# Ten tiles in two groups: the fourth output row of a tile is written directly behind the first, ahead of the second half of the next planes, and the last product of each of the two phases goes to another pair of PSUM banks

## What is computed

```
out = conv3x3_decomposed(x, lsq_quantize(w1, alpha1))
out = relu(batchnorm(out, gamma1, beta1))
out = conv3x3_decomposed(out, lsq_quantize(w2, alpha2))
out = batchnorm(out, gamma2, beta2)
out = relu(out + residual)          # residual = x
```

## Time and profile before

| | |
|---|---|
| median of three runs | 1582.2 us |
| the profiled execution | 1582.83 us, span 1580.7 us |
| phase 1 | to about 645 us |
| phase 2 | from about 645 to 1270 us |
| last stage | from about 1270 us on, DMA 99% busy |
| busy over the span | DVE 1196.5, PE 1112.5, ACT 842.3, POOL 497.5 us |
| granted TensorE clock | 0.887 of full speed over the span, 1.00 from 160 to 610 us and from 760 to 1260 us, 0.50 from 60 to 64 us and from 124 to 128 us |

### The profile page before, as it was taken

One profiled execution on the slowest core, in us unless ns is written; L12 is line 12 of the kernel. 1 busy time (PEld: TensorE's weight loads), 2 busy tenths in 40 slices (PEclk: granted clock), 3 DMA queues, 4 the chain that ended last, 5 costly groups with the idle time before them and its releaser, 6 DMA issues.

```text
span 1580.7 us, 22063 instructions
## 1 busy us (share of the span) xinstructions
PE 1112.5 (70%) x6954; PEld 1058.9 (67%) x6954; DVE 1196.5 (76%) x2074; ACT 842.3 (53%) x1135; POOL 497.5 (31%) x219
## 2 busy tenths in 40 slices
PE   5788998999999999579889999999989900000000
PEld 5787888888888888578888888888888900000000
DVE  7898998888888887688888888888888662323234
ACT  3454555555555555466766777776676552222224
POOL 2343334444433334133344444333344300000000
PEclk9998999999999999799999999999999955555555
DMA  4244444444442220001134444444222199999999
GB/s 191 84 164 161 164 163 163 163 163 180 181 182 107 81 81 1 1 41 82 81 122 163 163 183 180 177 184 189 103 81 81 51 419 430 429 430 430 430 430 407
DMA packets 28103, 296.89 MB, mean 188 GB/s; under 512 B 3888, under 2 KB 3888, under 8 KB 4784
## 3 DMA queue, kind: packets, MB, share of 16 engines
q1 hardware_dynamic: 22608, 245.25, 39.3%
q10 hardware_dynamic: 5472, 51.38, 7.6%
HBM read 174.59 MB, written 122.03 MB: 188 GB/s over the span
## 4 chain that ended last, share of the span: by engine, by line
DVE 42%; DMA 16%; PE 14%; issue 10%; DVEq 3%; ACT 2%; POOL 0%; POOLq 0%; ACTq 0%
PE conv_psum L942 13%; DMA slots<-conv_spill 10%; DVE slots L764 10%; DVE q_rows L696 8%; DVE v_rows L733 4%; DVE p_rows L721 4%; DVE d_lo L737 3%; DMA out<-slots 3%; DMA xbuf<-in_x 3%; DVE conv_psum L756 3%; DVE d L696 2%; DVE v_rows L696 2%; DVE slots L923 1%; DVE v_rows L717 1%; DVEq L764 1%
## 5 line engine op out<-in xcount | busy, mean ns | idle before, releaser
L454 POOL TENSOR_TENSOR v_lo<-v_rows,v_hi 128x1120 fp32r<-128x1120 f32 x192 | 494.9, 2592 | 751.8 <-ACT v_hi L513 751.8
L942 PE MATMUL conv_psum<-v_hi,w1T 128*128 128x284 f32 x1152 | 314.4, 301 | 69.2 <-DVE slots L764 62.5
L942 PE MATMUL conv_psum<-v_hi,w2T 128*128 128x284 f32 x1152 | 312.2, 299 | 66.5 <-DVE slots L764 58.9
L942 PE MATMUL conv_psum<-v_lo,w1T 128*128 128x284 f32 x1152 | 311.7, 299 | 0.0
L942 PE MATMUL conv_psum<-v_lo,w2T 128*128 128x284 f32 x1152 | 309.5, 297 | 0.0
L942 PEld LDWEIGHTS conv_psum<-v_hi,w1T 128*128 128x128 f32 x1152 | 222.0, 193 | 76.4 <-issue 70.5
L942 PEld LDWEIGHTS conv_psum<-v_hi,w2T 128*128 128x128 f32 x1152 | 220.7, 192 | 73.4 <-issue 63.2
L526 ACT COPY m<-conv_psum 128x568 f32<-128x568 f32 x128 | 81.3, 635 | 297.6 <-PE conv_psum L942 297.6
L556 ACT ACTIVATE squares<-slots,minus_shift 128x1120 bf16 (+3 forms) x192 | 223.5, 1164 | 28.8 <-DVE slots L764 15.1
L942 PEld LDWEIGHTS conv_psum<-v_lo,w1T 128*128 128x128 f32 x1152 | 222.6, 193 | 0.0
L942 PEld LDWEIGHTS conv_psum<-v_lo,w2T 128*128 128x128 f32 x1152 | 221.1, 192 | 0.0
(11 more groups left out here) (78 smaller groups left out, 1567.4 us busy)
## 6 DMA issues: line engine op xcount, KB each, us to landing
conv_spill<-slots SPq DMA_DIRECT2D x44, 1568.0 KB, 6.1
slots<-conv_spill SPq DMA_DIRECT2D x44, 1568.0 KB, 10.7
slots<-in_x SPq DMA_DIRECT2D x31, 1568.0 KB, 8.9
out<-slots ACTq DMA_DIRECT2D x30, 1568.0 KB, 11.6
xbuf<-in_x SPq DMA_DIRECT2D x28, 1568.0 KB, 52.8
xbuf_w<-in_x SPq DMA_DIRECT2D x4, 1568.0 KB, 51.9
out<-slots ACTq DMA_DIRECT2D x4, 784.0 KB, 10.3
slots<-in_L_conv_w SPq DMA_DIRECT2D x2, 576.0 KB, 9.7
```

The lines of the kernel that those rows point to most:

```text
L454: nc.gpsimd.tensor_tensor(pair_window(1, k), pair_rows(k), pair_window(0, k).bitcast(F32), ALU.subtract).then_inc(lo_ready[k], 1)
L942: last = nc.tensor.matmul(bank_run(M_BANK[k] + grp, G_TILES), w[:, M_WEIGHT[k] + kw, :], run(v_plane[half][k // 2], r0, r0 + G_TILES, kw - 1),
```

## The change

In every step but the last two of a phase, row 3 is written directly behind row 0, so ahead of p, v2, v3 and `d_lo` of the image after next. In the last step of a phase, product 5 goes to banks 2 and 3 and waits only for the copy of product 0 that lay there, not for the updates of the sums. The transposes of the second weights use banks 6, 7 and 0 in place of 2, 3 and 0, and all wait for the sums of the phase's last image.

```
-        W_BANK = [[0, 1, 4, 5], [2, 3, 0]]
+        W_BANK = [[0, 1, 4, 5], [6, 7, 0]]
...
-            def outer_row(g, p, b, j):
-                dve.wait_ge(outer_done, g * OD + (j + 1))
-                dve.wait_ge(sums_ready, g * SR + (SR - 1 + j))
-                row(g, p, b, (0, 3)[j], M_BANK[QUAD + j], 1.0, (s1, d1)[j], outer_rows_ready)
+            def outer_rows(g, p, b, last=False):
+                for j in range(2):
+                    dve.wait_ge(outer_done, g * OD + (j + 1))
+                    dve.wait_ge(sums_ready, g * SR + (SR - 1 + j))
+                    bank = LAST_BANK if last and j == 1 else M_BANK[QUAD + j]
+                    row(g, p, b, (0, 3)[j], bank, 1.0, (s1, d1)[j], outer_rows_ready)
...
-                    make_front(g + 2, p + 2, lambda: outer_row(g, p, b, 0))
+                    make_front(g + 2, p + 2, lambda: outer_rows(g, p, b))
                     lo_direct(g + 2, p + 2)
                 else:
-                    outer_row(g, p, b, 0)
-                outer_row(g, p, b, 1)
+                    outer_rows(g, p, b, last)
...
+            def outer_products(g, w, last=False):
                 pe.wait_ge(lo_ready[2], g + 1)
+                pe.wait_ge(sums_ready, g * SR + 2)
+                product(g, w, QUAD, M_BANK[QUAD]).then_inc(outer_done, 1)
+                if last:
+                    pe.wait_ge(m_copied, g * 2 + 1)
+                    product(g, w, QUAD + 1, LAST_BANK).then_inc(outer_done, 1)
+                else:
+                    pe.wait_ge(sums_ready, g * SR + SR)
+                    product(g, w, QUAD + 1, M_BANK[QUAD + 1]).then_inc(outer_done, 1)
...
             pe.wait_ge(w_int_ready[1], 2)
-            pe.wait_ge(m_copied, IMAGES * 2 - 1)
-            transpose_lot(1, 0)
-            transpose_lot(1, 1)
             pe.wait_ge(sums_ready, IMAGES * SR)
-            transpose_lot(1, 2)
+            for h in range(3):
+                transpose_lot(1, h)
```

More of the change, by code:

```diff
@@ L51, in residual_block @@
     CHUNK_BANK = [2, 3]
+    LAST_BANK = 2
     D_ROWS = H - WINO + 1
@@ L935, in transpose_lot, with product @@
                 last.then_inc(transposed, 1)
-            def product(g, w, k):
+            def product(g, w, k, bank):
                 for grp in range(GROUPS):
@@ L941, in product @@
                             r0 = (k % 2) * TILES + grp * G_TILES
-                            last = nc.tensor.matmul(bank_run(M_BANK[k] + grp, G_TILES),
+                            last = nc.tensor.matmul(bank_run(bank + grp, G_TILES),
                                                     w[:, M_WEIGHT[k] + kw, :],
@@ L965, in inner_products @@
                             pe.wait_ge(sums_ready, g * SR)
-                    product(g, w, k).then_inc(m_done, 1)
-            def outer_products(g, w):
+                    product(g, w, k, M_BANK[k]).then_inc(m_done, 1)
+            def outer_products(g, w, last=False):
                 pe.wait_ge(lo_ready[2], g + 1)
-                for j in range(2):
-                    pe.wait_ge(sums_ready, g * SR + (2, SR)[j])
-                    product(g, w, QUAD + j).then_inc(outer_done, 1)
+                pe.wait_ge(sums_ready, g * SR + 2)
[6 more added lines that the diff above has]
+                    product(g, w, QUAD + 1, M_BANK[QUAD + 1]).then_inc(outer_done, 1)
             taps = sorted(((kh, kw) for kh in range(3) for kw in range(3)), key=lambda t: t != (1, 1))
@@ L1021, in _ @@
             inner_products(IMAGES - 1, wT[0])
-            outer_products(IMAGES - 1, wT[0])
+            outer_products(IMAGES - 1, wT[0], last=True)
             pe.wait_ge(w_int_ready[1], 2)
-            pe.wait_ge(m_copied, IMAGES * 2 - 1)
-            transpose_lot(1, 0)
-            transpose_lot(1, 1)
             pe.wait_ge(sums_ready, IMAGES * SR)
-            transpose_lot(1, 2)
+            for h in range(3):
+                transpose_lot(1, h)
             pe.wait_ge(wT_ready, 2 * TAKES)
@@ L1037, in _ @@
             inner_products(STEPS - 1, wT[1])
-            outer_products(STEPS - 1, wT[1])
+            outer_products(STEPS - 1, wT[1], last=True)
 _INS = ["x", "L0_conv_w1", "L0_conv_alpha1", "L0_conv_gamma1", "L0_conv_beta1",
```

## The result

The changed kernel takes 1672.65 us (median of four runs, 1669.23 to 1674.34), the kernel before 1581.53 us on the same chip (four runs, 1580.83 to 1582.65). The ratio is 1.0573, 95% interval 1.0553 to 1.0593: **slower by 5.7%**. The profiled span is 1672.2 us against 1580.7, 91.5 us longer.

The account below looks back on a forecast made before the run. Before, a loop of product 3, VectorE's list to row 3 and product 2 bound, neither engine full; after, VectorE with blocked instructions. 1582.8 us with +44, +44, -8 and -5, together +75, gave 1658 us, range 1588 to 1700.

Parts of the forecast that it names:

- What the move gives: Steady step: row 3 stands 3.7 us earlier, TensorE's 1.69 us wait goes, VectorE's own work becomes 16.52 us.
- Two blocked instructions: Steady step: GpSimd's first instruction blocks v3 and its second `d_lo`, together 4.33 us; step 20.85 us.
- The step with a late TensorE: Step behind TensorE's idle gap: at the slow clock row 3 waits 0.9 us, one instruction is blocked, step 19.6 us.
- clock loss L: Products 2 and 3 at half clock behind TensorE's idle time: 1.94 us lost each time.
- phase 1, 25 steps: Steps from 130.37: 20 at 20.3 us and 5 at 21.3, 512.5 us against 468.2, +44.
- phase 2, 29 steps: All 29 steps at 20.3 us against 18.78, +44 us.
- first steps of the phases: Steps 0 to 3 of phase 1 some 4 us less, the first of phase 2 some 4 less: -8 us.
- phase ends: At a phase's end product 5 need not wait for the sums, so row 3 follows row 0; twice, -5 us.
- Weight steps: Five phase 1 steps with one more weight instruction and its chance of a block, 21.3 us each.
- clock stays up: Rival, chance 0.18: TensorE's 3.75 us gap does not lower the clock, every step is 20.85 us, total 1688 us.
- no block: Rival, chance 0.07: VectorE keeps the port between v3 and `d_lo`, TensorE binds at 17.1 us, total 1478 us.
- one block: Rival, chance 0.08: GpSimd's request falls inside v3, only `d_lo` is blocked, step 18.7 us, total about 1568 us.

## Why the prediction came out right, point by point

Forecast 1658 us, measured 1672.65, inside the range; slower by more than 0.2% had a chance of 0.83. Of the 91.5 us between the two profiled executions the sum had 75. The rest is made up of errors that point the same way (9.5 us in the steady steps, 2.4 in the first steps, 5 at the phase ends, and -0.3 at the start), so the total did not come near by large errors that cancel.

- **What the move gives**: right. TensorE's wait for the rows went, VectorE has no wait at line 749's place, and its own work came out as 16.41 us where 16.52 were forecast.
- **Two blocked instructions**: right in place and size. Forecast 4.33 us for the two, measured 2.20 + 2.16 = 4.36. The request comes 14.12 us behind the chunk (forecast 14.03), inside v2, and the chunk 1.10 us ahead of line 758 (forecast 1.09: 500.97 to 502.07). The two-block step is 20.77 us against 20.85 forecast, TensorE's idle time 3.70 against 3.75. In the changed kernel `d_lo` takes 3.30 to 3.36 us in all 49 steady steps (from 271 and from 759 us on). The Trainium skill (SBUF — State Buffer, Who interferes with whom) says that the later one blocks until the earlier ends. The totals that took 1.74 us and ended with GpSimd's third instruction agree with it. One block added 2.2 us, 0.2 less than a whole GpSimd instruction (2.40 in the earlier trace rows), which is what the prediction had made of that rule; why it is less no run here shows. The prediction gave the rule as if every instruction with at most one SBUF input were left alone. The section excepts some, those in a 2-port perf mode, and the last section here shows a VectorE instruction with one SBUF input that was blocked.
- **The step with a late TensorE**: the mechanism is right (rows wait, one block, short gap, then a two-block step again), the size is off. The term was a clock loss L of 1.94 us, taken from products 2 and 3 behind 60.51. Here the slow stretch lies in the chunks and lasts from 500.97 to beyond 506 us, and chunk to GpSimd's request grows from 14.12 to 517.44 - 500.97 = 16.47 us: L is 2.35. The rows wait 0.70 + 0.73 = 1.43 us where 0.9 was forecast, so the step is 20.2 and not 19.6. The mean of the pair is 20.49 us; the forecast took 20.3. The prediction had named a case near this one (a loss of 2.5 us or more gives 20.5) and chose below it. L is not one number either: the run with row 3 alone has three such steps of 19.4 us, below the 19.6 of the forecast.

The sum term by term, from line 758 at the same steps as the earlier trace rows, the rows of the changed kernel for steps 4, 29, 31, 32, 33, 62 and 63:

```profile
128.52 0.75 DVE L758 TENSOR_TENSOR conv_psum<-m,conv_psum 128x568 f32<-128x568 f32 x1
645.19 0.74 DVE L758 TENSOR_TENSOR conv_psum<-m,conv_psum 128x568 f32<-128x568 f32 x1
684.29 0.76 DVE L758 TENSOR_TENSOR conv_psum<-m,conv_psum 128x568 f32<-128x568 f32 x1 [1.71 <-PE conv_psum L945]
723.00 0.75 DVE L758 TENSOR_TENSOR conv_psum<-m,conv_psum 128x568 f32<-128x568 f32 x1 [1.13 <-ACT m L528]
744.50 0.74 DVE L758 TENSOR_TENSOR conv_psum<-m,conv_psum 128x568 f32<-128x568 f32 x1
1338.11 0.74 DVE L758 TENSOR_TENSOR conv_psum<-m,conv_psum 128x568 f32<-128x568 f32 x1
1354.11 0.76 DVE L758 TENSOR_TENSOR conv_psum<-m,conv_psum 128x568 f32<-128x568 f32 x1 [1.74 <-PE conv_psum L945]
```

| part | forecast | measured |
|---|---|---|
| phase 1, 25 steps to 645.19 | +44 | 516.67 against 468.21: +48.5 |
| phase 2, 29 steps to 1338.11 | +44 | 593.61 against 544.61: +49.0 |
| first steps of the phases | -8 | 0 to 3: -1.5; first of phase 2: -4.1 |
| phase ends | -5 | +3.4 (29 to 31), -2.6 (31 to 32), -0.8 (62 to 63): 0.0 |
| together, with -0.3 at the start | +75 | +91 |

- **Weight steps**: forecast 21.3 us each, measured 21.35, the mean of the five from 128.52 to 235.28 us. Right in the mean; the single steps are 20.7 to 22.6 us, and the prediction showed no working for the 1.0 us that it added, so the close agreement is in part luck.
- **First steps**: 4 us were forecast for steps 0 to 3 and 1.5 came. The two steps with long stalls did shorten (25.83 to 22.35, 25.26 to 21.06), but the two between them grew (18.63 to 22.34, 20.53 to 22.99). In the second step of phase 1 `d_lo` was blocked (3.34 us) and the weight instruction behind it as well, in the third p (3.24) and v2 with v3 (3.45). The term left that out. The first step of phase 2 gave its 4.
- **Phase ends**: the term counted a saving by the banks, 2.5 us at each end. At the boundary between the phases 2.6 us came. At the end of phase 2 they gave 0.4 us in the kernel with the banks alone; the 0.8 us in the table (62 to 63) are not theirs, since that step is 16.00 us with row 3 moved and the old banks too, and 16.81 with the banks alone. And the term forgot that the steps 29 and 30, before the last of phase 1, carry the blocks too: 39.10 us against 35.66.

The rival **clock stays up** came true in the phase 1 of the experiment with more matmuls: every step 20.82 us where 20.85 was forecast for it. The rival **no block** fell: between v3 and `d_lo`, issued back to back, GpSimd got in in all 49 steady steps, since `d_lo` was blocked in each. The rival **one block** was seen in phase 2 of the same experiment, at 19.20 us and with a TensorE that the extra matmuls kept full; the changed kernel never settled there.

## What to carry to other kernels

When two-operand SBUF instructions of VectorE are moved, lay GpSimd's work beside the new order before anything else: an edit that takes away a 1.7 us wait cost 5.7% here, because it moved two instructions 0.74 us later, under GpSimd. The cure is not fewer waits but one more: start GpSimd's run behind the last VectorE instruction it excludes and let it end under instructions that read PSUM; and price a move in a loop by where the loop settles, not by its first step (here 18.7 us for the first by the prediction's working, and a measured 20.8 and 20.2 in turn once the late `d_lo` holds TensorE and with it the request's place). After such a cure try the rejected move again: it was worth -57 us with the wait and +91 without.

## What the runs showed of the hardware that I had not expected

- An instruction's size does not protect it. The totals of 128 x 13 elements waited 1.57 us for a GpSimd instruction (1.74 us against 0.17).
- Nor does a single SBUF operand protect every instruction. In the second step of phase 1 of the changed kernel the weight instruction, which reads `slots` alone, was held behind GpSimd; with no GpSimd instruction running it takes 0.76 us:

```profile
8.83 0.76 DVE L284 TENSOR_SCALAR slots<-slots 128x1152 f32<-128x1152 f32 x1
80.17 2.94 DVE L284 TENSOR_SCALAR slots<-slots 128x1152 f32<-128x1152 f32 x1
```

- The extra matmuls left one run with two ways of running, each steady through its phase: 20.82 us a step in phase 1, with VectorE blocked twice, and 19.20 us in phase 2, with TensorE full. They are told apart by whether GpSimd's request falls ahead of v3 or behind it.
- By the comparison with phase 1 of that run, the halved clock did not lengthen the run of the changed kernel: the steps in which TensorE started at 1.2 GHz are its shorter ones (20.2 against 20.8 us), since the late rows move v2 and v3 out of GpSimd's way.
- One thing stays open: in the kernel with `d_lo` first, the steady steps drift between 20.13 and 20.52 us in pairs and even ones, with the clock at 0.98 from 160 to 560 us. I did not follow that up.
